# A chain of four weight-building layers: the LoRA products on 64 rows, issued as alternating pairs, and two low parts moved on VectorE

## The reference

```python
# layer 0: a plain weight, and a sign mask scaled by one coefficient per batch
x + x @ W0.T + b0 + (x @ (2 * mask - 1)) * coeff
# layer 1: a weight quantized to a codebook of 8 levels, with a LoRA delta of rank 64
lora_delta = lora_B @ lora_A * 0.5
normalized = (weight + lora_delta) / scale      # per row and group of 128 columns
w_eff = cb[searchsorted(thresholds, normalized)] * scale + lora_delta
x + x @ w_eff.T
# layers 2 and 3: a plain weight with per-batch adapters of rank 16, and adapters alone
```

## Time and profile before

| | us |
|---|---|
| median of 3 runs | 549.23 |
| lowest, highest | 548.74, 549.58 |
| the profiled execution's own time | 549.03 |
| its span | 547.4 |
| set-up, until `load_w0t` is issued | 169.13 |

### The profile page before, as it was taken

How to read it: one execution, slowest core, us unless ns; L and a number is a source line. 1 busy time by engine, 2 the same in 40 slices (tenths; PEclk the granted TensorE clock), 3 DMA queues, 4 the chain that set the end, 5 groups by cost and what they waited for, 6 DMA issues and landing times.

```text
span 547.4 us, 9005 instructions
## 1 busy us (share of the span) xinstructions
PE 531.3 (97%) x2864; PEld 458.2 (84%) x2864; DVE 461.2 (84%) x742; ACT 350.7 (64%) x681; POOL 169.0 (31%) x170
## 2 busy tenths in 40 slices
PE   4899999999999999999999999999999999999997
PEld 4898788888888788888888888888888888888886
DVE  5997898988865879987999889897897987989853
ACT  3776775776745774675767657666676665766730
POOL 2669767987734320003004003000300400400120
PEclk9999999999999999999999999999999999999999
DMA  8767031833395993458446455746845645564222
GB/s 228 247 86 152 24 117 43 255 128 125 89 208 167 356 333 61 151 185 173 131 141 188 92 179 168 124 151 193 160 135 152 175 101 182 169 108 154 77 50 77
DMA packets 147281, 82.57 MB, mean 151 GB/s; under 512 B 105060, under 2 KB 124516, under 8 KB 147124
## 3 DMA queue, kind: packets, MB, share of 16 engines
q1 hardware_dynamic: 145444, 78.34, 52.1%
q0 software_dynamic: 1520, 3.86, 2.7%
q10 hardware_dynamic: 288, 0.01, 0.0%
HBM read 65.93 MB, written 16.26 MB: 150 GB/s over the span
## 4 chain that ended last, share of the span: by engine, by line
PE 75%; DVE 11%; DMA 4%; ACT 4%; SPq 3%; issue 2%; DVEq 0%; ACTq 0%
PE bank L1679 17%; PE bank L1686 9%; PE bank L1723 5%; PE bank L1722 5%; PE bank L1553 5%; PE bank L1721 5%; PE bank L1555 5%; PE bank L1554 5%; PE bank L1772 3%; PE bank L1770 3%; PE bank L1771 3%; DVE merged_ring L1207 3%; PE bank L1734 2%; DVE m_lo L1213 2%; PE bank L1463 2%; DMA mask_ring<-in_mask_Bx4096x_ik 2%
## 5 line engine op out<-in xcount | busy, mean ns | idle before, releaser
L1679 PE MATMUL bank<-x_t_pair,m_hi 128*128 128x512 f32 x512 | 128.8, 394 | 1.9 <-ACT m_hi L820 1.7
L605 POOL TENSOR_TENSOR x_t_pair<-x_sum,x_t_pair 128x256 fp32r<-128x256 f32 x32 | 29.8, 959 | 290.9 <-ACT x_t_pair L893 290.9
L1679 PEld LDWEIGHTS bank<-x_t_pair,m_hi 128*128 128x128 f32 x512 | 92.6, 189 | 19.9 <-ACT m_hi L820 3.1
L820 ACT CAST m_hi<-merged_ring 128x512 fp32r<-128x512 f32 x128 | 73.0, 619 | 51.0 <-PE bank L1686 25.7
L810 ACT ACTIVATE merged_ring<-mask_ring,batch_now 128x1024 f32<-128x1024 int32 x64 | 78.1, 1243 | 25.1 <-DMA mask_ring<-in_mask_Bx4096x_ik 24.3
L1213 DVE TENSOR_TENSOR m_lo<-merged_ring,m_hi 128x512 fp32r<-128x512 f32 x128 | 84.6, 709 | 9.1 <-ACT m_hi L820 9.0
L1207 DVE TENSOR_TENSOR merged_ring<-merged_ring,w_t 128x1024 f32<-128x1024 f32 x64 | 76.4, 1221 | 14.3 <-ACT merged_ring L810 13.3
L1686 PEld LDWEIGHTS bank<-x_t_pair,m_lo 128*128 128x128 f32 x512 | 69.9, 191 | 5.0
L1686 PE MATMUL bank<-x_t_pair,m_lo 128*128 128x256 f32 x512 | 71.5, 283 | 0.0
L1723 PE MATMUL bank<-P_hi,x_t_pair 128*128 128x496 f32 x160 | 61.5, 385 | 0.0
L1722 PE MATMUL bank<-P_lo,x_t_pair 128*128 128x496 f32 x160 | 61.5, 384 | 0.0
(11 more groups left out here) (221 smaller groups left out, 1110.2 us busy)
## 6 DMA issues: line engine op xcount, KB each, us to landing
mask_ring<-in_mask_Bx4096x_ik SPq DMA_DIRECT2D x64, 512.0 KB, 4.4
w_nat<-in_L_cond_W SPq DMA_DIRECT2D x14, 512.0 KB, 5.1
x_t_squares<-in_x SPq DMA_DIRECT2D x56, 128.0 KB, 3.0
w_raw<-in_L_cond_weight SPq DMA_DIRECT2D x16, 256.0 KB, 4.8
out<-out_staged SPq DMA_DIRECT2D x16, 248.0 KB, 5.5
w0t_dram<-w_out SPq DMA_DIRECT2D x14, 256.0 KB, 2.7
w_t<-w0t_dram SPq DMA_DIRECT2D x6, 512.0 KB, 5.0
g_batch<-g_dram POOLq DMA_DIRECT2D x21, 128.0 KB, 4.2
```

Of the source, the lines that this page charges most:

```text
L820: nc.scalar.copy(Mh[:, n % MR], ring_f[:, k % MR, h * HALF:(h + 1) * HALF]).then_inc(s["h_set"], 1)
L1679: mm(bank[L0_BANK[HT * h + j]][:, :], Mh[:, n % MR, j * P:(j + 1) * P], xThl[:, :, :, k + i, :], start=(k + i == 0), stop=False, skip_grou ...
```

## The change

1. **64 rows, alternating.** `lbt` becomes 128x512: rows 0 to 63 hold lora_B's transpose for h = 0, rows 64 to 127 that for h = 1. `la` gets a second copy of lora_A on rows 64 to 127 (POOL, two copies behind its first indirect DMA). The two memsets go. Four transposes of 128x128 instead of eight of 128x64, and one ACT copy instead of two. lora_B comes in two DMAs instead of one.
2. **Pairs.** `delta_pair(q)` issues both halves' products in turn: h = 0 on rows 0 to 63, h = 1 on rows 64 to 127, four times. It stands at the start, where `delta(2)` was, at t = 2 of groups 0 and 1, and at t = 0 of groups 2 to 5.
3. **Banks and a copy.** All even halves but the first use bank 5, the odd ones 4 and 3 in turn. For q = 1 to 6 ACT copies the even half's product to SBUF (`delta_copy`, 128x512, behind `norm(2q+1)`), and `effective(2q)` reads `dkept` instead of the bank. The next pair waits for that copy and for `effective(2q-3)`.
4. **VectorE's order.** `add_delta(0)` goes ahead of the steps and thresholds. From `half(6)` on `half(n)` with even n keeps only part 0 of `p_lo`; parts 1 and 2 move into `terms_a` of the next half, behind its first and second term. `gsum(1)` moves from the end of `half(7)` to behind the first term of `half(8)`.
5. **SP** waits for `eff_set` 13 too before it loads x over the tiles.

```diff
-    lbn = at("lb_nat", [P, KT, RL], F32, lo + 28 * KB)
+    lbn = at("lb_nat", [P, HT, 2, RL], F32, lo + 28 * KB)
...
-    lbt = at("lora_b_t", [P, D], F32, reg_b2)
+    lbt = at("lora_b_t", [P, HALF], F32, reg_b2)
+    dkept = at("delta_kept", [P, HALF], F32, reg_b2 + 2 * KB)
...
+        KEEP_FROM = 1
         def dps(n):
-            return bank[3 + n % 3]
+            if n % 2:
+                return bank[3 + (n // 2 + 1) % 2]
+            return bank[5 if n else 3]
...
-        DELTA_STEPS = {0: (2, 6), 1: (2, 5)}
+        DELTA_STEPS = {0: 2, 1: 2}
...
-            sp.dma_start(lbn[:, :, :], lora_b.rearrange("(t p) r -> p t r", p=P)).then_inc(s["lora_b_in"], 16)
+            for h in range(2):
+                sp.dma_start(lbn[:, :, h], lora_b.rearrange("(h t p) r -> h p t r", h=2, p=P)[h]).then_inc(s["lora_b_in"], 16)
...
             sp.wait_ge(s["delta_done"], 2 * G)
+            sp.wait_ge(s["eff_set"], 2 * G - 3)
             load_x(0)
...
+            pool.wait_ge(s["lora_a_in"], 16)
+            for cols in (slice(0, 2 * P), slice(2 * P, D)):
+                nc.gpsimd.tensor_copy(la[RL:2 * RL, cols], la[0:RL, cols]).then_inc(s["lora_a_up"], 1)
+            pool.wait_ge(s["lora_a_up"], 2)
...
+            def delta_copy(q):
+                act.wait_ge(s["raw_used"], 2 * q + 1)
+                if q > KEEP_FROM:
+                    act.wait_ge(s["eff_set"], 2 * q - 1)
+                nc.scalar.copy(dkept[:, :], dps(2 * q)[:, :]).then_inc(s["delta_kept"], 1)
...
-            for h in range(2):
-                act.wait_ge(s["lbt_tr"], h + 1)
-                nc.scalar.mul(lbt[0:RL, h * 512:(h + 1) * 512], bank[5 + h][0:RL, :], L1_SCALE).then_inc(s["lbt_set"], 1)
+            act.wait_ge(s["lbt_tr"], 1)
+            nc.scalar.mul(lbt[:, :], bank[5][:, :], L1_SCALE).then_inc(s["lbt_set"], 1)
...
             mid_up(2)
+            delta_copy(1)
...
+                if n % 2 == 0 and 2 * KEEP_FROM <= n < 2 * G - 2:
+                    delta_copy(n // 2)
...
-            nc.vector.memset(la[RL:P, :], 0.0).then_inc(s["lora_pad"], 1)
-            nc.vector.memset(lbt[RL:P, :], 0.0).then_inc(s["lora_pad"], 1)
...
             nc.vector.reciprocal(rs[:, :, :], sc[:, :, :]).then_inc(s["recip_set"], 1)
+            add_delta(0)
...
+                behind = (n - 5) // 2 if n % 2 and n > 6 else None
+                if behind is not None:
+                    p_lo(behind, range(1, 2))
+                if n == 8:
+                    gsum(1)
...
+                if behind is not None:
+                    p_lo(behind, range(2, 3))
...
-                ins = nc.vector.tensor_tensor(acc[:, h], pooled[:, h], dps(n)[:, :], ALU.add)
+                kept = h == 0 and KEEP_FROM <= q < G - 1
+                if kept:
+                    dve.wait_ge(s["delta_kept"], q + 1 - KEEP_FROM)
+                ins = nc.vector.tensor_tensor(acc[:, h], pooled[:, h], dkept[:, :] if kept else dps(n)[:, :], ALU.add)
...
-                if n == 7:
-                    gsum(1)
...
-                    p_lo((n - 4) // 2)
+                    p_lo((n - 4) // 2, range(1))
...
+            def delta_half(n, t):
+                q, rows = n // 2, slice(n % 2 * RL, (n % 2 + 1) * RL)
+                return mm(dps(n)[:, t * P:(t + 1) * P], lbt[rows, t * P:(t + 1) * P], la[rows, q * P:(q + 1) * P],
+                          start=(t == 0), stop=True, skip_group_check=True)
+            def delta_pair(q):
+                if q == 0:
+                    pe.wait_ge(s["lora_a_up"], 1)
+                    pe.wait_ge(s["lbt_set"], 1)
+                elif q == 1:
+                    pe.wait_ge(s["eff_set"], 1)
+                else:
+                    if q == 2:
+                        pe.wait_ge(s["lora_a_up"], 2)
+                    pe.wait_ge(s["delta_kept"], q - KEEP_FROM)
+                    pe.wait_ge(s["eff_set"], 2 * q - 2)
+                for t in range(HT):
+                    for h in range(2):
+                        ins = delta_half(2 * q + h, t)
+                        if t == HT - 1:
+                            ins.then_inc(s["delta_done"], 1)
...
-                    if t in DELTA_STEPS.get(g, (0, 5)):
-                        m = 2 * g + 4 + t // HT
-                        if m < 2 * G:
-                            delta(m)
+                    if t == DELTA_STEPS.get(g, 0) and g + 2 < G:
+                        delta_pair(g + 2)
...
                 comp(0, t, *w1_split(g))
-                if t == KT - 2:
+                if t in (0, KT - 2):
                     return
-                if t == 0:
+                if t == 1:
                     pe.wait_ge(s["p_ready"], 3 * (g - 1) + 2)
-                if t == KT - 1:
+                if t in (1, KT - 1):
                     comp(1, t - 1, *w1_split(g))
```

More of the change, by code:

```diff
@@ L222, in cond_resid_chain @@
             s_set v_set h_set m_ready m_used l0_done x1_part x1_sum x1_hi x1_ready0 x1_ready1 x_turned xt_hi xt_first xt_later xt_ready u_done u_part u_summed u_hi u_ready
-            out_done out_added out_st0 out_st1 out_st2 out_st3 c_in gl_in c_stored lora_pad now_set coef_now
+            out_done out_added out_st0 out_st1 out_st2 out_st3 c_in gl_in c_stored delta_kept lora_a_up now_set coef_now
             t_step t_summed t_hi t_ready a_summed a_hi a_ready prod_done c_sums c11_set out_copied b2_split side_set side_done side_step side_st""".split()}
@@ L965, in _, with add_delta @@
             nc.vector.memset(now_tab[:, :, :], 0.0).then_inc(s["ub_zero"], 1)
-            nc.vector.memset(la[RL:P, :], 0.0).then_inc(s["lora_pad"], 1)
-            nc.vector.memset(lbt[RL:P, :], 0.0).then_inc(s["lora_pad"], 1)
+            def add_delta(n):
+                q, h = n // 2, n % 2
+                dve.wait_ge(w1_in[h], 16 * (q + 1))
+                dve.wait_ge(s["delta_done"], n + 1)
+                flat = raw[:, h].rearrange("p t c -> p (t c)")
+                nc.vector.tensor_tensor(flat, flat, dps(n)[:, :], ALU.add).then_inc(s["raw_used"], 1)
             dve.wait_ge(s["tok_in"], 32)
@@ L1008, in _ @@
             link(nc.vector.tensor_tensor(c(4), c(4), c(5), ALU.min))
[L1010 to L1016, removed]
             def term(i, dst):
@@ L1132, in _ @@
             W0_EYES = {6: 0, 8: 1, 9: 2, 10: 3, 12: 4, 14: 5}
-            add_delta(0)
+            add_delta(1)
             nc.vector.tensor_scalar(cs[:, :, :], sc[:, :, :], cb[:, 0:1], None, ALU.mult).then_inc(s["first_level"], 1)
-            add_delta(1)
             dve.wait_ge(s["ident_set"], 1)
@@ L1445, in _ @@
             pe.wait_ge(s["ident_set"], 1)
-            pe.wait_ge(s["lora_b_in"], 16)
-            for h in range(2):
-                for t in range(HT):
[L1450 to L1465, removed]
+            pe.wait_ge(s["lora_b_in"], 32)
+            for t in range(HT):
+                ins = nc.tensor.transpose(bank[5][:, t * P:(t + 1) * P], lbn[:, t].rearrange("p h r -> p (h r)"), ident[:, :])
+            ins.then_inc(s["lbt_tr"], 1)
+            def delta_half(n, t):
[13 more added lines that the diff above has]
+                    pe.wait_ge(s["eff_set"], 2 * q - 2)
+                for t in range(HT):
+                    for h in range(2):
+                        ins = delta_half(2 * q + h, t)
+                        if t == HT - 1:
+                            ins.then_inc(s["delta_done"], 1)
             def w0_transpose(blk, h):
@@ L1478, in w0_transpose @@
                 ins.then_inc(s["w0_tr"], 1)
[L1480 to L1483, removed]
+            delta_pair(0)
             def w2_transpose(t):
@@ L1538, in _ @@
             v_part(4)
-            delta(2)
+            delta_pair(1)
             w2_transpose(5)
@@ L1545, in _ @@
             v_part(7)
-            delta(3)
             COLS = [(0, 512), (512, 1024), (1024, EXT)]
```

## The result

The changed kernel takes 552.48 us (median of 6 runs, 551.26 to 554.03) against 549.10 for the kernel before on the same chip (6 runs, 548.74 to 549.90): a ratio of 1.0056, interval 1.0042 to 1.0071. It is 3.4 us slower, where 2.0 faster was forecast; the time lies inside the range given, next to its upper end. The profiled execution took 552.44, with a span of 550.5.

What follows compares the result with a forecast made beforehand. PE, busy 97% of the span, was taken as the bound. Start +0.7, SBUF reading +0.8, ACT copy +0.5, pairs -4.0 sum to -2.0: 549.03 - 2.0 + 0.2 = 547.2 us, range 545.6 to 552.6.

Steps and rivals of the forecast that it cites:

- Part by part: The prediction's section that priced each changed part up to load_w0t; its terms sum to -2.0 us.
- rival two: Set-up groups: DVE, ACT and POOL hold PE, which gains 2.2, not 4.0; -0.2, so 549.0 us; chance 0.20.
- start: Start, up to w1's block: DVE's first term at 14.2 against 13.51, so all that follows is 0.7 us late.
- keep: Even product kept in SBUF: 0.8 us for DVE's waits on POOL plus 0.5 for the ACT copy.
- the sum's 0.8 and 0.5: 0.8 us: effective(2q) waiting for POOL, first at 51.17; 0.5 us: ACT's copy delaying PE in group 1.
- `effective(2q)` from SBUF and the copy: DVE waits out running POOL operations, 0.8 us (0 to 2.1); ACT's delta_copy adds 0.5 (0 to 0.57).
- Waiting once or twice: DVE's first SBUF effective and the identity square behind it wait for POOL: 0 to 2.1 us less slack, taken as 0.8.
- in DVE's spare time: The other five SBUF effective, 3.2 us on average, cost nothing: DVE 92.1 busy of some 100 in the groups.
- The saving of 4.0: PE behind 62.40: nine delta, 8.0 us, become four pairs of 1.0, 4.0 (saving bounds 4.4 and minus 0.6).
- Rival three: PE's pairs: the row halves don't overlap, a pair takes 1.78 + 0.1; +3.3, so 552.5 us; chance 0.25.
- Costed at nothing: Memsets, DVE's two moved low parts, gsum(1) one term later and SP's added wait: 0 us each.

Runs made afterwards that it cites:

- single halves: Kernel before with the 64-row layout alone, one half at a time: 552.56 us; with the ACT copy and the SBUF reading too: 557.67.
- psum_read_no_copy: Changed kernel with effective(2q) reading the odd half's PSUM bank and without delta_copy (wrong delta in even halves): 547.54 us, ratio 0.9967 to the kernel before.
- no_copy_lo_back: psum_read_no_copy with DVE's low parts back at the end of the even half: 550.15 us, ratio 0.9996 to the kernel before.
- b2_first: Changed kernel with ACT's second copy of b2's transpose, b2_set(1), put ahead of w1_hi(2): 552.62 us.
- no_copy_in_turn: psum_read_no_copy with each pair's four products on rows 0 to 63 ahead of the four on 64 to 127: 550.73 us, ratio 1.0025 to the kernel before.
- psum_read: Changed kernel with effective(2q) reading the odd half's PSUM bank, copy and waits kept (wrong delta in those halves): 549.56 us, ratio 1.0001 to the kernel before.

## Why the prediction was wrong

The forecast failed in two steps of "Part by part", and the mechanism of rival two was in part there. The sum's own terms, at `load_w0t`, beside what was measured:

| term | forecast | measured | from |
|---|---|---|---|
| start | +0.7 | +0.6 to 0.9 | `norm(1)` 21.55 (21.00), block of w1 issued at 45.84 (44.97), one execution each |
| keep, ahead of `a3_transpose(1)` | +1.3 | +2.1 to 2.6 | single halves with and without it, 2.55, of which 0.44 is the start's |
| keep, behind it | 0 | +1.0 | 105.39 against 104.41 |
| products, `delta(7)` to `delta(15)` | -4.0 | -2.9 | 9 x 0.89 = 8.0 to 4 x 1.28 = 5.1 |
| PE waits for `w_out` | 0 | +1.6 | 106.73 - 2.9 + 1.6 = 105.4 |
| low parts moved | 0 | -1.0 | 105.39 against 104.41 |
| half 7 now ahead of `a3_transpose(1)` | 0 | +0.4 | 1.28 - 0.89 |
| sum | -2.0 | +1.8 to 2.6 | 2.58 seen |

The "keep" is the sum's 0.8 and 0.5 together. The times differ by 3.4: the 0.5 behind `load_w0t` and 0.3 outside the span are in no line of the sum, and nor is the fall of the granted clock, which the prediction didn't have at all. That the sum comes near 2.58 is in part chance, as the lines ahead of `a3_transpose(1)` move with the execution. Counted from the issue of w1's block, which takes the start out, that point comes after 17.43 in the kernel before, 18.36 in `psum_read_no_copy` and 20.48 in the changed kernel, so the keep is 2.1 of it here too. The line on the waits for `w_out` is worked out as what the second part lacks. In that part the trace of `no_copy_lo_back` shows this wait alone; that nothing else is in the line is argued, not shown by a run of its own:

```profile
PE bank L1505 <- ACT w_out L713: 1.6, 2, 1.0
```

*The step that failed most is `effective(2q)` from SBUF and the copy.* The mechanism was right, DVE waiting out POOL, and so was the first place, half 3. The size was not. "Waiting once or twice" was taken as 0.8 net of the slack, but DVE waited twice and nearly in full: 1.61 and 1.23 instead of 0.68 and 0.29, 1.9 us, inside the bound of 2.1 that I had. POOL's sums run one behind the other there, so DVE's second operation meets the next of them. Then I let the other five cost nothing "in DVE's spare time": 88.9 busy of 100 is spare on average only. DVE's operations stand in a loop with POOL's and ACT's for one NORM bank, and in the changed kernel that loop is on the chain from 102.72 to 114. Together the keep costs 4.9 in place of 1.3, and part of that comes with the fall of the granted clock, which 29 of 35 runs with the keep have (see `b2_first`).

*The saving of 4.0.* A pair was to take 0.99. The overlap is whole, as forecast, but the two changes of mode cost 0.39 and not 0.1, just over the bound of 0.38 that I had given for them: four pairs cost 1.2 more. Another 1.6 of it PE stood waiting for ACT's copies of W0's squares. That is rival two, the loop of DVE, ACT and POOL, under which PE was to gain 2.2; it gained 1.34 behind 66.32.

*Rival three* (no overlap) gave the time almost exactly, 552.5, and was wrong in its mechanism: a pair of 16 MATMULs takes 1.29, not 1.88. That the number agrees is chance.

*The start* agrees in size by luck and was wrong in reason. In the eleven executions with the new start w1's block is issued anywhere from 43.88 to 46.74 (44.97 and 44.82 with the old one), so no size of 0.7 can be told from it. DVE's first term came at 12.78, not at 14.2: POOL reached the indirect DMA at 5.74 instead of 7.75, so its two copies of lora_A were early. `norm(1)` was later all the same, since its chain now goes through the adapters' DMA, landing at 13.62, and PE's transposes of layer 2's weight.

*Costed at nothing:* the memsets and SP's wait, rightly as far as any view shows. The moved low parts were not nothing but a gain of 1.0 here and 0.9 alone. With pairs most of it is a shorter wait of PE for `w_out` (0.8 of 0.98); that they come off the end of the even half would fit this and isn't shown.

## What to carry to other kernels

Before a product is kept in SBUF to free a bank, ask which other engine reads SBUF at that moment: an addition of two SBUF tiles on VectorE costs a GpSimd operation's rest on top whenever it begins amid one (five of six here), and a loop over three engines turns that into time even where VectorE is idle a tenth of it. When an edit takes away a fall of the granted clock, look through the whole execution before you acquit the clock: here it had moved from 56 us to 192. Row halves of the array do overlap wholly, but only pay where both are issued in one piece: entering and leaving costs 0.39 us, so a lone 64-row half is dearer than a padded 128-row one (1.28 against 0.89). And take a change with several parts apart: its smallest part, a reordering of the low parts, was the only one for which a run shows a gain as it stood.

## What the runs showed of the hardware that I had not expected

- Zero padding was the faster form: four products on 64 rows took 1.28 with 128-row products around them, on 128 rows 0.89.
- With PE idle in 54 to 56 us, the granted clock of the changed kernel fell behind it and came back by itself while PE was full; the stretches (columns as above) show it:

```profile
54.00:56.00 2.00, 0.00 (x0) 0.00 (x0) 2.00 (x3) 1.14 (x4) 1.12 (x2) 1.00 0.44 131
56.00:58.00 2.00, 1.88 (x8) 1.64 (x9) 2.00 (x4) 2.00 (x7) 1.77 (x2) 0.71 0.00 0
58.00:60.00 2.00, 2.00 (x6) 1.56 (x5) 1.64 (x3) 1.41 (x3) 1.48 (x2) 0.50 0.02 4
60.00:62.00 2.00, 2.00 (x12) 1.73 (x12) 1.09 (x4) 0.96 (x2) 1.44 (x2) 0.94 0.00 0
```

- The products at the level of 0.50 stand 0.43 apart instead of 0.23. In `b2_first` PE stood 2.4 us until 60.37 and the granted clock read 1.00 until 66; it fell behind a wait of 1.9 at 191.45. In the changed kernel a wait of 1.6 until 192.09 was followed by 1.00.
- Products on the two row halves don't keep their order. In `no_copy_in_turn` at 77.42 the second half's first three products start (77.97, 78.19, 78.30) before the last one of the first half (78.30, known by its semaphore), which was issued ahead of them. This is why a pair in turn takes 1.84 and not twice 0.89 and 0.39.
- `norm(1)` begins anywhere from 20.84 to 22.95 over the executions with the new start. POOL's first operation on layer 2's weight doesn't explain it: at 11.61 and 11.73 it is nearly the same in `psum_read_no_copy` and `psum_read`, and `norm(1)` is at 20.92 and 22.95. What does is open. The changed kernel spreads more (551.26 to 554.03) than the one before in the same batch (548.74 to 549.90); its slowest run has the lowest mean granted clock, 0.993 against 0.997.
